# Decoder kernel, state space stage: where the own rows are added to the level sums

## The reference

```python
B = x @ B_w.T + B_b;  C = x @ C_w.T + C_b          # one group for all heads
dt = jax.nn.softplus(x @ dt_w.T + dt_b)
dA = dt * A                                        # A = -exp(A_log)
L = jnp.exp(segsum(dA))                            # decay from token s to token l
...
Y = (Y_diag + Y_off).reshape(b, t, h, p) + D[None, None, :, None] * xh
return Y.reshape(b, t, d) @ out_w.T + out_b
```

## Time and profile before

| | us |
|---|---|
| median of 3 runs (lowest, highest) | 1306.26 (1300.8, 1311.11) |
| the profiled execution | 1298.79 |
| its span | 1296.8 |
| TensorE busy in the span | 1198.7 (92%) |
| VectorE busy | 948.4 (73%) |
| ScalarE busy | 698.1 (54%) |
| GpSimd busy | 471.9 (36%) |
| mean granted TensorE clock | 0.98 |

### The profile page before, as it was taken

How to read it: one execution, slowest core, us unless ns; L and a number is a source line. 1 busy time by engine, 2 the same in 40 slices (tenths; PEclk the granted TensorE clock), 3 DMA queues, 4 the chain that set the end, 5 groups by cost and what they waited for, 6 DMA issues and landing times. The chain is left out here.

```text
span 1296.8 us, 25738 instructions
## 1 busy us (share of the span) xinstructions
PE 1198.7 (92%) x9194; PEld 918.0 (71%) x9194; DVE 948.4 (73%) x1746; ACT 698.1 (54%) x1335; POOL 471.9 (36%) x553
## 2 busy tenths in 40 slices
PE   6999997998888768998899999999997999999998
PEld 5676764343444647896678888787886888888887
DVE  7899986799998477985768677777776567455555
ACT  3778763788888455002565656656654463333332
POOL 2444642466664134865543324233242201112210
PEclk9999998899999998999999999999998999999999
DMA  5111161134331300003100000000000200000001
GB/s 179 35 37 38 44 151 35 42 82 98 82 95 34 109 10 1 1 0 109 44 8 4 8 4 4 8 4 8 28 1 1 74 25 25 26 25 25 2 1 65
DMA packets 60701, 50.94 MB, mean 39 GB/s; under 512 B 9064, under 2 KB 52936, under 8 KB 60232
## 3 DMA queue, kind: packets, MB, share of 16 engines
q1 hardware_dynamic: 60622, 49.88, 13.9%
HBM read 37.93 MB, written 11.53 MB: 38 GB/s over the span
## 5 line engine op out<-in xcount | busy, mean ns | idle before, releaser
L209 DVE TENSOR_REDUCE stacks_neg_max<-psum 128x2 f32<-128x512 f32 x256 | 164.0, 685 | 29.1 <-PE psum L205 28.1
L977 ACT ACTIVATE fa_probs<-psum 128x1024 f32<-128x1024 f32 x128 | 130.7, 1023 | 36.0 <-PE psum L1102 35.9
L2102 POOL TENSOR_TENSOR ga_probs<-ga_probs,ga_top 128x1024 f32<-128x1024 f32 x16 | 30.5, 1906 | 203.7 <-DVE ga_top L2279 203.7
L2697 ACT ACTIVATE mo_silu<-psum 128x512 f32<-128x512 f32 x64 | 38.3, 598 | 115.0 <-PE psum L1960 115.0
L205 PE MATMUL psum<-stacks_k_stack,stacks_q_stack 48*128 48x256 bf16 x512 | 89.7, 283 | 9.9 <-DVE stacks_neg_max L209 6.5
L2825 DVE TENSOR_TENSOR mo_mid<-mo_silu,psum 128x512 f32<-128x512 f32 x64 | 43.9, 686 | 74.2 <-ACT mo_silu L2697 74.1
L1102 PE MATMUL psum<-stacks_q_stack,stacks_k_stack 51*128 51x256 bf16 x512 | 86.7, 280 | 0.0
L2091 POOL TENSOR_TENSOR ga_q_scaled<-ga_q,ga_q_inv 128x1024 f32<-128x1024 f32 x32 | 70.1, 2190 | 40.3 <-ACT ga_q_inv L2145 40.3
L205 PEld LDWEIGHTS psum<-stacks_k_stack,stacks_q_stack 48*128 48x128 bf16 x512 | 32.7, 96 | 64.2 <-DVE stacks_neg_max L209 36.4
L2829 DVE TENSOR_TENSOR mo_mid_low<-mo_mid,mo_mid_high 128x512 fp32r<-128x512 f32 x64 | 45.0, 703 | 43.9 <-ACT mo_mid_high L2688 43.9
L2138 ACT ACTIVATE ga_q_scaled<-ga_q 128x512 f32<-128x512 f32 x64 | 40.3, 632 | 61.8 <-DVE ga_q L2252 61.8
(11 more groups left out here) (493 smaller groups left out, 3776.0 us busy)
## 6 DMA issues: line engine op xcount, KB each, us to landing
k_parts<-da_k_parts SPq DMA_DIRECT2D x96, 64.0 KB, 2.0
stacks_k_stack<-k_parts SPq DMA_DIRECT2D x32, 192.0 KB
q_parts<-stacks_parts SPq DMA_DIRECT2D x48, 64.0 KB, 2.0
stacks_q_stack<-q_parts SPq DMA_DIRECT2D x32, 96.0 KB
x<-in_x SPq DMA_DIRECT2D x4, 512.0 KB, 6.2
da_context<-in_ctx SPq DMA_DIRECT2D x4, 512.0 KB, 7.6
stacks_q_stack<-q_parts SPq DMA_DIRECT2D x32, 64.0 KB
fa_context<-in_ctxT SPq DMA_DIRECT2D x16, 128.0 KB, 2.3
```

Source lines behind the costliest of these rows:

```text
L209: return core.nc.vector.tensor_reduce(self.neg_max[:, b, :, head_at(h)], core.psum[:, bank, :].rearrange("p (q k) -> p q k", q=2), AX.X, A ...
L977: nc.scalar.activation(probs[:, g].rearrange("p h k q -> p h (k q)"), ps[:, 2 + 2 * (g % 2):4 + 2 * (g % 2), :], ACT.Exp).then_inc(exp_don ...
```

## The change

VectorE gets one more instruction for each tile, behind L1762: it adds own_rows to the first of the three blocks of sums, in place (128x256). It waits for the sums (its own engine's L1762) and for own_rows (GpSimd), and signals a new semaphore `own_added`. TensorE's product of own_rows with the identity is taken out, so three products a half remain; TensorE waits for `own_added` where it waited for `own_ready`. GpSimd's own_rows waits, before it overwrites a buffer, for `own_added` of two tiles back where it waited for `y_psum`.

```diff
--- before.py
+++ after.py
@@ -1315,8 +1315,8 @@
         soft_abs, soft_step, tail_exp, tail_log, rate_ready, dA_ready, spans_psum, decay_ready, decay_dt_ready, own_step, own_done = (
             sem(n) for n in ("soft_abs", "soft_step", "tail_exp", "tail_log", "rate_ready", "dA_ready", "spans_psum", "decay_ready",
                              "decay_dt_ready", "own_step", "own_done"))
-        inputs_ready, own_ready, biased, level_ready, level_psum, outputs_ready, sums_ready, y_psum, yT_ready, out_psum, x_ready, stats_done = (
-            sem(n) for n in ("inputs_ready", "own_ready", "biased", "level_ready", "level_psum", "outputs_ready", "sums_ready",
+        inputs_ready, own_ready, own_added, biased, level_ready, level_psum, outputs_ready, sums_ready, y_psum, yT_ready, out_psum, x_ready, stats_done = (
+            sem(n) for n in ("inputs_ready", "own_ready", "own_added", "biased", "level_ready", "level_psum", "outputs_ready", "sums_ready",
                              "y_psum", "yT_ready", "out_psum", "x_ready", "stats_done"))
         F_LOADS, WEIGHT_LOADS, LOADS = 4 * 16, 4 * 16, 6 * 16
         Q_PIECE, Q_PIECES = 512, KC * Q_COLS // 512
@@ -1427,7 +1427,7 @@
                     if isinstance(t, int) and t + 1 in (0, 3):
                         pool.wait_ge(own_done, S_GROUPS if t + 1 else 1)
                     if started(t, 1):
-                        pool.wait_ge(y_psum, t)
+                        pool.wait_ge(own_added, t)
                     nc.gpsimd.tensor_tensor(by_head(own_rows[:, place(1)]), by_head(xn_kept[:, t + 1, :]), per_head(own[:, t + 1, :]),
                                             ALU.mult).then_inc(own_ready, 1)
 
@@ -1760,6 +1760,9 @@
                                             decay[:, t, :, :, None].to_broadcast([P, LEVELS, S_HEADS, S_HD]), ALU.mult).then_inc(outputs_ready, 1)
                     dve.wait_ge(outputs_ready, t + 1)
                     nc.vector.tensor_tensor(sums[:, place(0)], outputs[:, 0:LEVELS // 2], outputs[:, LEVELS // 2:], ALU.add).then_inc(sums_ready, 1)
+                    dve.wait_ge(sums_ready, t + 1)
+                    dve.wait_ge(own_ready, t + 1)
+                    nc.vector.tensor_tensor(sums[:, place(0), 0], sums[:, place(0), 0], own_rows[:, place(0)], ALU.add).then_inc(own_added, 1)
                 if valid(t + 2) and started(t, 0):
                     scores_by_level(t + 2, place(2))
                 if valid(t - 1):
@@ -1932,16 +1935,15 @@
                                                 start=(c == 0), stop=(c == KC - 1))
                     done.then_inc(out_psum, 1)
                 if valid(t):
-                    pe.wait_ge(own_ready, t + 1)
                     pe.wait_ge(sums_ready, t + 1)
+                    pe.wait_ge(own_added, t + 1)
                     if isinstance(t, int) and t == 0:
                         pe.wait_ge(scores_ready, S_GROUPS)
                     for c in range(KC):
                         columns = slice(c * P, (c + 1) * P)
                         y = ps[:, 6, columns]
-                        nc.tensor.matmul(y, own_rows[:, place(0), columns], ident[:], start=True, stop=False)
                         for m in range(LEVELS // 2):
-                            done = nc.tensor.matmul(y, sums[:, place(0), m, columns], ident[:], start=False, stop=(m == LEVELS // 2 - 1))
+                            done = nc.tensor.matmul(y, sums[:, place(0), m, columns], ident[:], start=(m == 0), stop=(m == LEVELS // 2 - 1))
                     done.then_inc(y_psum, 1)
 
             pipeline(pe, turn, 2)
```

## The result

The changed kernel takes 1323.83 us (median of 4 runs, 1318.97 to 1327.48) against 1304.07 us of before in the same runs: ratio 1.0144, 95% interval 1.0114 to 1.0174, some 19 us slower. The forecast was slower, 1337 us, in a range of 1322 to 1362. Measured again beside other kernels the ratio was 1.0207 (1.0168 to 1.0246).

What follows compares the result with a forecast made beforehand. TensorE was taken to set the pace. Thirteen turns at 2.36 us more gave 30.7 us, the last two +1, ties taking off about as much: +31 us on the 1306.26 us median, 1337 us, range 1322 to 1362.

Steps and rivals of the forecast that it cites:

- TensorE bound, 0.45 us a tile: TensorE sets the steady pace; dropping four of 16 identity products saves 0.45 us a tile, its turn falling to 4.79 us.
- The addition's own duration, 0.42 us: VectorE's added 128x256 addition, behind L1762, takes 0.42 us alone, with bounds of 0.29 to 0.98 us.
- Taking turns: VectorE instructions with two SBUF inputs and GpSimd's exclude each other; inputs hold 2.72 us, the addition 0.28 us.
- the theory: VectorE and GpSimd take turns, and the change lets GpSimd's 2.72 us inputs in between L1762 and L1696.
- A blocked turn, 7.6 us: GpSimd's inputs fall between L1762 and the addition, so a turn takes 7.6 us in place of 5.24.
- the branch: The loop branches every second turn between L1771 and L1758 on VectorE, taking 0.59 in place of 0.34 us.
- The near tie: If the addition goes before inputs, the next turn's L1762 waits behind inputs: two turns in 13.86 us, 6.9 each.
- The number of blocked turns: All 13 turns from tile 0 to tile 13 are blocked, each costing 2.36 us, 30.7 us in all.
- a rival that could only cost: TensorE falls to half clock for most of the stage: 9.6 us turns, 57 us more, 1363 us; chance 0.10.
- No blocking: Rival: VectorE bounds the pipeline at 5.05 us a turn, 15 turns give -3 us, 1303 us; chance 0.13.
- Half of the turns: Rival: unblocked turns of 5.05 us alternate with blocked ones of 7.6, +14 us, 1320 us; chance 0.08.
- The last two turns, +1 us: With no inputs left, two additions may stand behind GpSimd's L1405 pieces, 1.47 us each, against 0.9 saved on TensorE: +1 us.

Runs made afterwards that it cites:

- no_own: The kernel before with TensorE's product of own_rows left out and nothing in its place (own terms missing from the output); ratio to before 1.0032.
- inputs_late: The changed kernel with one more GpSimd wait: inputs of tile t+2 wait for VectorE's addition of tile t; ratio to before 1.0097.
- gate_before: The changed kernel with one more GpSimd wait: inputs of tile t+2 wait for VectorE's addition of tile t-1; ratio to before 1.0006.
- filler: The changed kernel with four unneeded identity products on TensorE in each turn but the first, 0.88 us more work a tile; ratio to before 1.0057.
- swapped: The changed kernel with GpSimd's two instructions of a turn in the other order, own_rows before inputs; ratio to before 1.0025.
- half_inputs: The changed kernel with GpSimd's inputs for only three of the six levels, so the output is wrong; ratio to before 1.0072.
- before_again: The kernel before, unedited, run once more for a second profile; ratio to before 0.9985, stage 88.87 us.
- again: The changed kernel, unedited, run once more for a second profile; ratio to before 1.0207, stage 107.59 us.
- add_only: The kernel before with VectorE's addition beside it, into a spare tile nothing reads; TensorE unchanged, GpSimd's own_rows also wait for the addition; ratio to before 1.0166.
- split_inputs: The changed kernel with GpSimd's inputs as two instructions of three levels each, TensorE waiting for the second; ratio to before 1.016.

## Why the prediction was right, and where its size was off

**TensorE bound, 0.45 us a tile.** Right for before, and the size too: in no_own level products start at 545.70, 550.49 and 555.29, 4.79 us apart. Taken away, the 0.45 us are worth nothing (no_own), as forecast.

**The addition's own duration, 0.42 us.** It measured 0.42 to 0.43 us in every turn in which it met nothing; the worked-out 0.42 was right. L1696 behind it is issued 0.34 us after it.

**Taking turns.** The worked-out 2.72 and 0.28 us came out as 2.71 and 0.28: in the timeline above inputs get their turn at L1762's end, 551.73, and end at 554.44, the addition at 554.72. inputs_late, gate_before, filler, swapped and half_inputs leave VectorE's work as it is and change when or how long GpSimd holds, and each moves the time the way the theory had it.

**A blocked turn, 7.6 us.** Seven of the 13 turns from tile 0 to tile 13 are blocked ones, of 7.44 to 7.88 us, 53.48 us in all: 7.64 on average, where 7.6 was worked out. In the timeline above, with x = 554.72, the end of the addition, L1758 starts at x + 1.96 and L1762 at x + 3.76 (worked out, with the branch: 1.95 and 3.73), and inputs are issued at x + 4.58 (worked out: 4.48).

**The near tie.** Worked out wrong. Where the addition wins, the forecast had the next inputs meet L1762, and two turns in 13.86 us. Measured are 7.88 and 7.68, and 7.56 and 7.65 us: 15.56 and 15.21. The working left out that TensorE's level products wait for L1696 (1.86 us at 577.38); the next inputs come 6.72 us behind the addition's end (573.80 to 580.52), not 4.62, and meet the addition once more. So ties took nothing off, and the 9 us that the range allowed for them were not what made the time shorter.

**The number of blocked turns: the term that was off.** The sum had 13, 2.36 us each, 30.7 us; measured were 7, and six others of 5.67 us on average, 87.49 us in all against 67.88 before: 19.6 us, of which the seven cost 16.9 and the six 2.7. The six are of two kinds. The first three (3.98, 7.60, 4.87) and one that follows an unblocked one (5.12) are where the cycle has not set in; the forecast took it from the first turn on. (The 7.60 us are a wait of L1771 for TensorE, and before_again has 3.53 and 8.24 us in that place.) Two, of 6.47 and 5.97 us, have TensorE at the lower clock for a part. I had that as a rival that could only cost: in fact, while the blocking lasts, a slower TensorE lets GpSimd's inputs start later, behind L1696, and **saves** a blocked turn. Pauses of 2.7 and 2.9 us in TensorE's work came ahead of both. again has the same in four turns (6.48, 5.94, 5.94 and 5.70 us, with level products of 4.40 to 4.55 us); in no_own, add_only and split_inputs, with a granted clock of 1.00 from 540 to 600 us, the blocked turns, once they set in, follow one another with none between. So each of the six free turns that follow a blocked one has slow TensorE records (in the one of 5.97 us, identity products of 2.78 and level products of 3.24 us), and those three kernels at the full clock have no such turn. No run changed the clock alone, though, and why it fell here and not in split_inputs, where TensorE is busy for even less of the time (30.39 of 44 us), stays open.

**The range and the rivals.** The measured 1323.83 us lie in the range by 2 us. Its lower end had been set by ties and by the spread of the runs, and neither is why fewer turns were blocked: that the time fell inside was luck in part. No blocking (1303 us) is refuted by the durations of the addition. Half of the turns (1320 us), which had a chance of 0.08, was nearer the measured time than my forecast and right by the count: 7 of 13 turns are blocked here and 6 of 13 in again. The order does differ from turn to turn by more than the branch's 0.25 us, which was its condition.

**The last two turns, +1 us.** They came to +0.9 us (6.00 and 5.16 against 5.02 and 5.25), but not as worked out: the addition of 1.38 us behind L1405 stands in the turn of 5.16, and the turn of 6.00 has L1771 wait 1.14 us for TensorE, whose level products last 3.90 us in it. The size was right by luck.

## What to carry to other kernels

Before moving work between engines, write down for one turn who asks for the shared resource when, counted from one event, and see what the change moves in that order; here either half of the change, 0.45 us off TensorE or 0.46 us onto VectorE, let a 2.7 us GpSimd instruction in front of VectorE's chain. An engine that looks like the bound may be what keeps the others apart: taking load off TensorE gained nothing (no_own), and putting load on it helped the changed kernel (filler). Where two engines take turns, fix the order with a wait rather than trust the pace, and try where it goes: one turn early it took away the whole loss (gate_before, 1.0006), one turn later about half (inputs_late, 1.0097 beside 1.0207).

## What the runs showed that I had not expected

Turns with slow level products were the shorter ones, as told above. And the queueing moves time ahead of the pipeline too, in unchanged code: in the changed kernel's profile two instructions for the own factors meet GpSimd's inputs:

```profile
517.53 2.90 POOL L1423 TENSOR_TENSOR fs_inputs<-fs_xn_kept,fs_decay_dt 128x1536 f32<-128x1536 f32 x1
517.65 3.33 DVE L1678 TENSOR_TENSOR fs_same<-fs_scoresT,ident 128x512 f32<-128x512 f32 x1
...
521.43 2.85 POOL L1423 TENSOR_TENSOR fs_inputs<-fs_xn_kept,fs_decay_dt 128x1536 f32<-128x1536 f32 x1
521.74 2.69 DVE L1683 TENSOR_TENSOR fs_own<-fs_dt,fs_same_dot 128x128 f32<-128x128 f32 x1
...
524.67 1.75 DVE L1758 TENSOR_TENSOR fs_work<-psum,fs_decay 128x1536 f32<-128x1536 f32 x1
```

L1678 and L1683 take 0.69 and 0.29 us when alone and 3.33 and 2.69 here, and the first L1758 starts at 524.67 in place of 516.29. The change has no part in it: before_again has the same two records (3.33 and 2.69 us) and starts its first L1758 at 523.77, again has them too and starts it at 519.03. This start varies between executions of the same code, and the 8.4 us by which the first two profiles differ there are not part of the stage's 20.4 us.
